# Macaron block (feed-forward, attention, feed-forward): bias row, gamma and beta scaled on ScalarE, and the bias of the first six tiles added in two transfers

## What is computed

```python
x = x + 0.5 * ffn(_layernorm(x))
x = x + attn(_layernorm(x))          # 16 heads of 32, causal
x = x + 0.5 * ffn(_layernorm(x))

# ffn(x):
z = x_flat @ ternary_quant(W_syn).T + b_syn        # 2048 hidden units
topv, _ = jax.lax.top_k(z, k)                      # k = 204 of 2048 in each row
hidden = jnp.where(z >= topv[:, -1:], jax.nn.relu(z), 0.0)
out = hidden @ ternary_quant(W_out).T + b_out
return layernorm(x + out, gamma, beta)
```

## Time and profile before

| | |
|---|---|
| median of 3 runs | 1203.69 us (1200.65 to 1203.73) |
| the profiled execution | 1203.05 us |
| its span, first to last instruction | 1201.3 us |
| mean granted clock of TensorE, share of full | 0.969 |
| busy: TensorE, VectorE, ScalarE, GpSimd | 88%, 74%, 67%, 31% |
| bias transfers | 32 of 1024 KB, median 8.0 us from issue to landing |

### The profile page before, as it was taken

The page is one execution under the profiler, slowest core; times in us unless marked ns, Lnnn a source line. Parts: engine busy times, 40 slices in busy tenths (PEclk is TensorE's granted clock), DMA queues, the critical chain, the costliest instruction groups (busy, mean ns, idle before and its releaser), DMA issues. The chain is left out here.

```text
span 1201.3 us, 17848 instructions
## 1 busy us (share of the span) xinstructions
PE 1059.9 (88%) x5862; PEld 476.8 (40%) x5862; DVE 890.0 (74%) x2207; ACT 803.6 (67%) x1193; POOL 376.2 (31%) x406
## 2 busy tenths in 40 slices
PE   0677899998889789999999699999999799998886
PEld 0233455554444333232244233232344345554443
DVE  4867899999985787885243787884225889999893
ACT  5368988898743546566713556667646988999762
POOL 1311254544554041100220041102211134544456
PEclk9898899998999989999999989999999899999999
DMA  9445333233000225200001143210043433344000
GB/s 367 126 89 102 71 71 58 54 67 67 27 1 1 53 63 115 54 37 2 1 4 36 36 101 77 54 37 2 1 83 76 88 71 71 72 88 89 19 19 35
DMA packets 28105, 74.62 MB, mean 62 GB/s; under 512 B 5332, under 2 KB 7767, under 8 KB 23255
## 3 DMA queue, kind: packets, MB, share of 16 engines
q0 software_dynamic: 7456, 39.33, 17.5%
q1 hardware_dynamic: 20536, 33.99, 8.9%
HBM read 56.37 MB, written 4.21 MB: 50 GB/s over the span
## 5 line engine op out<-in xcount | busy, mean ns | idle before, releaser
L859 ACT ACTIVATE arena<-arena,X 128x2048 int8<-128x2048 f32 x154 | 307.9, 2005 | 18.3 <-issue 10.4
L919 ACT ACTIVATE arena<-zP,asc 128x512 f32<-128x512 f32 (+3 forms) x384 | 200.7, 582 | 110.9 <-PE zP L706 80.0
L549 PE MATMUL zP<-T,arena 128*128 128x512 f16 x1024 | 248.1, 393 | 0.0
L597 PE MATMUL oP<-T,arena 128*128 128x512 f16 x832 | 199.9, 384 | 0.9 <-DVE arena L1438 0.9
L549 PEld LDWEIGHTS zP<-T,arena 128*128 128x128 f16 x1024 | 103.3, 101 | 125.6 <-issue 16.9
L815 ACT ACTIVATE arena<-zP,sc 128x512 f32<-128x512 f32 x128 | 87.0, 686 | 69.9 <-PE zP L549 69.7
L597 PEld LDWEIGHTS oP<-T,arena 128*128 128x128 f16 x832 | 81.7, 99 | 80.2 <-issue 6.3
L702 PE MATMUL zP<-arena 98*128 98x512 f16 (+3 forms) x384 | 110.8, 334 | 0.9 <-ACT arena L919 0.7
L1124 POOL TENSOR_TENSOR arena<-arena 128x512 f32<-128x512 f32 x16 | 20.3, 1271 | 257.7 <-DVE arena L1582 235.9
L1552 DVE CUSTOM_DVE_ANT_0 scored<-hP,causal 128x128 bf16<-128x128 f32 (+3 forms) x170 | 80.9, 485 | 21.5 <-PE hP L681 20.2
L681 PE MATMUL hP<-arena 96*128 96x512 f16 (+3 forms) x256 | 83.6, 345 | 14.3 <-DVE mx L1552 11.0
(11 more groups left out here) (206 smaller groups left out, 1797.6 us busy)
## 6 DMA issues: line engine op xcount, KB each, us to landing
arena<-bz_row POOLq DMA_DIRECT2D x32, 1024.0 KB, 8.0
arena<-arena SPq DMA_DIRECT2D x168, 64.0 KB, 2.0
arena<-in_w_synT SPq DMA_DIRECT2D x4, 1024.0 KB, 8.1
arena<-in_w_outT SPq DMA_DIRECT2D x4, 1024.0 KB, 14.9
x_sb<-in_b_o POOLq DMA_DIRECT2D x2, 2048.0 KB, 17.9
out_dram<-x_sb SPq DMA_DIRECT2D x16, 256.0 KB, 2.0
x_sb<-in_x SPq DMA_DIRECT2D x3, 1024.0 KB, 13.9
arena<-in_w_o SPq DMA_DIRECT2D x2, 1024.0 KB, 5.2
```

Of the source, the lines that this page charges most:

```text
L549: mm = pe.matmul(zP[:, c * CW:(c + 1) * CW], part[:, g % 2, k, :], T1[:, k, c * CW:(c + 1) * CW], start=(n == 0 and k == 0), stop=(n == 1 ...
L597: mm = pe.matmul(o, part[:, k, :], T2[:, k, :], start=(c == 0 and n == 0 and k == 0), stop=False)
L859: act.activation(junk[:, counted[0] % 2, :], Z[:, g % ZR, :], ACT.Sign, bias=X[:, 2, k:k + 1], accum_out=S[:, k:k + 1]).then_inc(sm["cnt"], 1)
L919: act.activation(PT[:, m // 4 % 2, h, q0:512], colP[m % 3][:, q0:512], ACT.Exp, scale=asc[:, g, 10:11]).then_inc(sm["exp_done"], 1)
```

## The change

The bias row, gamma and beta are scaled by ScalarE instead of GpSimd: gamma and beta ahead of the absolute sum of the last weight piece, the bias row behind the sum of squares. For the first six tiles of pass 0 the bias is added in two transfers: columns 0 to 1535 (chunks 0 to 2) as soon as three chunks are evacuated, issued ahead of the root of that slot, and columns 1536 to 2047 one slot later, ahead of the next first part. From tile 6 on everything is as before. The semaphore `z_set` becomes two, for even and odd tiles.

```diff
+        SPLIT_BIAS = 6
+        def bias_parts_of(g):
+            return ((0, 3), (3, 4)) if g < SPLIT_BIAS else (None, (0, 4))
+        def z_ready(g):
+            mine = range(g % 2, g + 1, 2)
+            return sm[f"z_set{g % 2}"], 16 * sum(2 if m < SPLIT_BIAS else 1 for m in mine)
...
                 for c in range(4):
+                    if (n, c) == (1, 3):
+                        act.wait_ge(sm["vec_in"], 32)
+                        for v in (gam, bet):
+                            act.activation(v[:, :], v[:, :], ACT.Copy, scale=0.5).then_inc(sm["vec_set"], 1)
                     act.wait_ge(sm[f"w{n + 1}_in{c}"], 16)
...
             act.wait_ge(sm["sq_done"], 1)
+            act.wait_ge(sm["bsyn_in"], 16)
+            act.activation(bz, bsyn[0:1, :], ACT.Copy, scale=SH[0:1, :]).then_inc(sm["bz_set"], 1)
...
-            def add_bias(f, i):
-                g = f * NT + i
-                if (f, i) == (0, 0):
+            def add_bias(f, i, part):
+                g = f * NT + i
+                if not bias_parts_of(g)[part]:
+                    return
+                lo, hi = bias_parts_of(g)[part]
+                if (g, part) == (0, 0):
                     pool.wait_ge(sm["bz_out"], 16)
-                pool.wait_ge(sm["z_evac"], 4 * g + 4)
-                pool.dma_start(Z[:, g % ZR, :], bz_row.partition_broadcast(P), accum_op=ALU.add).then_inc(sm["z_set"], 16)
+                pool.wait_ge(sm["z_evac"], 4 * g + hi)
+                cols = slice(lo * CW, hi * CW)
+                pool.dma_start(Z[:, g % ZR, cols], bz_row[cols].partition_broadcast(P), accum_op=ALU.add)\
+                    .then_inc(sm[f"z_set{g % 2}"], 16)
...
                     do(final, f, s, S_FIN + 1)
+                    if f == 0 and s - 2 < SPLIT_BIAS:
+                        do(add_bias, f, s, 2, 1)
                     do(rstd2, f, s, S_FIN)
+                    late = f * NT + s - 1 >= SPLIT_BIAS
+                    if not late:
+                        do(add_bias, f, s, 1, 0)
                     if f == 0 or s > 0:
                         do(rstd1, f, s, -1)
-                    do(add_bias, f, s, 1)
+                    if late:
+                        do(add_bias, f, s, 1, 1)
                     if f == 0 and s == 0:
-                        pool.wait_ge(sm["scales_set"], 1)
-                        pool.tensor_scalar(bz, bsyn[0:1, :], SH[0:1, :], None, ALU.mult).then_inc(sm["bz_set"], 1)
 
                         pool.wait_ge(sm["scales_set"], 3)
                         pool.tensor_tensor(SIG, sc[:, 16:17], half[:, :], ALU.pow).then_inc(sm["scales_set"], 1)
-                        link(pool.tensor_scalar(gam[:, :], gam[:, :], 0.5, None, ALU.mult))
-                        link(pool.tensor_scalar(bet[:, :], bet[:, :], 0.5, None, ALU.mult))
+                        pool.wait_ge(sm["vec_set"], 2)
```

More of the change, by code:

```diff
@@ L294, in program @@
                  "ones_set ident_set consts_set abs_done sum_ps sum_read tern_done sq_done scales_set search_set "
-                 "bz_set bz_out z_set orow_in bcol_in bpart_set brow_out bones_set "
+                 "bz_set vec_set bz_out z_set0 z_set1 orow_in bcol_in bpart_set brow_out bones_set "
                  "stats1 xn_done rstd1 xT_ps xT_hi xT_lo z_ps z_evac upd cnt below_set ok_set ok_sum ok_read "
@@ L851, in count @@
                     act.wait_ge(sm["search_set"], 1)
-                    act.wait_ge(sm["z_set"], 16 * (g + 1))
+                    act.wait_ge(*z_ready(g))
                 if s >= FIRST_UPD:
@@ L1330, in count_here @@
                 g = f * NT + i
-                dve.wait_ge(sm["z_set"], 16 * (g + 1))
+                dve.wait_ge(*z_ready(g))
                 after(0)
```

## The result

The changed kernel takes 1189.95 us (median, 1188.85 to 1190.24) against 1202.72 for the kernel before, run beside it: ratio 0.9897 with a 95% interval of 0.9885 to 0.9909. Its profiled span is 1187.0 us (before 1201.3), its mean granted clock 0.978 (before 0.969). The forecast was 1192.3 in a range of 1189 to 1198. Run a second time, beside another set of the kernel before, it took 1191.97 (1188.7 to 1194.8), ratio 0.9911 (0.9896 to 0.9927). So the gain is 10.9 to 12.8 us; 11.4 was forecast. It is small, 1.0% of the time, but both intervals leave out 1.

The account below looks back on a forecast made before the run. The first slots' chain was taken as the bound: VectorE's stall beside GpSimd's scaling, then counts waiting for bias transfers. 5.8 + 5.4 = 11.2 us off 1203.05 gives 1191.9, from the median 1192.5; forecast 1192.3, range 1189 to 1198.

Parts of the forecast that it names:

- The stall goes: Start-up: `normal` of tile 1 no longer held beside GpSimd's scaling; 5.77 us gained at the transposes of tile 2.
- the charge of gamma and beta: Start-up: scaling them on ScalarE takes 1.3 us and delays the first `mm1` by some 0.8 us, beside `normal`.
- Slot 2: VectorE's `update` starts directly behind `normal` at 58.5, no longer waiting for the count: 1.2 us gained, 6.97 in all.
- no delay, 0.8 to spare: Slot 2: the part ahead of tile 3's root is issued by 56.1; the root wants to start at 56.9.
- rival 1: Slots 2 to 4: root behind the evacuation costs more, matmuls at TensorE's lower level; 3.6 us lost, 1197, chance 0.17.
- Slots 3 to 6: Waits for the count go: slot 3 gains 2.62, slot 4 0.46, slot 5 nothing, slot 6 1.15; 11.2 in all.
- The transfers: Bias transfers, issue to landing: a quarter 4.0 us, three quarters 6.7 us (estimates), landing before ScalarE needs them in slot 2.
- rival 4: Slots 5 and 6: TensorE idles less and keeps its higher level; 2 to 3 us more gained, 1189.5, chance 0.07.
- Rival 3: Five slots: GpSimd's issues held up by VectorE push the root; 27 us lost against 11.2, 1219, chance 0.04.
- Rival 2: Only the start-up pays, bias landing as late as now: 1197.9, or 1200.8 if that saving is halved; chance 0.05.

Follow-up runs that it names:

- e5: Changed kernel with the bias row alone scaled on GpSimd again in one instruction, gamma and beta staying on ScalarE: 1194.87 us, ratio 0.9934.
- e13: Changed kernel with gamma and beta scaled behind the bias row instead of ahead of the last absolute sum: 1191.33 us, one run.
- e3: Changed kernel with the bias split after two chunks instead of three, two transfers of 1024 columns (halves): 1189.97 us, ratio 0.9888.
- e9: Changed kernel with the bias split after one chunk instead of three, 256 KB ahead and 768 KB behind: 1190.29 us, ratio 0.9899.
- e4: Changed kernel with the first bias part issued behind the root instead of ahead of it: 1191.50 us, ratio 0.9904.
- e8: Changed kernel without an edit, timed and profiled again: 1191.97 us, ratio 0.9911.
- the second profiles: Changed kernel and kernel before, each profiled once more without an edit: 1191.97 us (ratio 0.9911) and 1203.60 us (one run).
- e2: Changed kernel with bias row, gamma and beta scaled on GpSimd again, keeping only the two bias transfers: 1199.51 us, ratio 0.9970.
- e10: Changed kernel with bias in halves and tile 2's mean, variance, root and normalize moved ahead of the search's start values: 1194.03 us, ratio 0.9924.
- e1: Changed kernel with the bias of every tile in one transfer again, keeping only the scaling on ScalarE: 1197.57 us, ratio 0.9951.
- e11: Changed kernel with the bias row scaled on GpSimd in two instructions of 1x1024: 1192.18 us, one run.
- e6: Changed kernel with the bias row scaled on GpSimd in four instructions of 1x512: 1192.45 us, ratio 0.9918.

## Why the prediction was right, and where not

**The stall goes: right, 0.39 too small.** 5.77 was summed, 6.16 came. e5 shows that the bias row alone carries 5.35 of it at the transposes of tile 2, and 4.3 of the 10.66 at slot 7. `x_lo` of tile 1 was at 41.06 (forecast 41.3), the charge of gamma and beta 0.56 (forecast 0.8) and hidden, which e13 confirms. The bias row took 2.00 us on ScalarE (forecast 1.91). By the Trainium skill, "ScalarE: Activation LUTs", section What ACT_TABLE_LOAD costs, an instruction with one pointer operand takes about 280 ns and 0.833 ns for each element, 1.99 us for the row (an estimate by that page); the trace agrees with 2.00.

**Slot 2: the term that was off.** The step "no delay, 0.8 to spare" failed. The 32 matmuls took 8.35 us at a granted clock of 0.82, behind 2.92 us of idle time; chunk 2 was evacuated at 56.4 instead of 55.1, and the root of tile 3 started at 57.29 instead of 56.9 and read 0.35 longer. The slot gained 0.24 (6.16 to 6.40) where 1.20 was forecast. That is rival 1's mechanism in one slot, not in three, and it cost 1.0 us, not 3.6. e3 shows which part of it the root's wait costs. Its window of the same stretch has the same clock; its transposes take 1.11 us and its 32 matmuls 8.08:

```profile
49.80:58.50 8.70, 8.58 (x35) 4.15 (x36) 5.69 (x8) 4.29 (x6) 1.97 (x4) 0.82 0.66 120
```

```profile
49.92 1.11 PE L543 MATMUL xP<-identf,arena 128*128 128x128 f32 x4 [3.32 <-DVE arena L1301]
...
51.70 0.69 DVE L1307 SCALAR_TENSOR_TENSOR arena<-xP,arena 128x512 f16<-128x512 f32 x1 [1.84 <-ACT arena L800]
```

Its roots wait for two chunks only, and its `update` comes at 58.45, 0.62 earlier than in the changed kernel. So the root behind chunk 2 costs 0.6 of the 1.0 us. The rest stands before it: in e3 `x_lo` starts 1.78 us behind the start of the transposes (49.92 to 51.70) where it was 1.32 before (56.07 to 57.39), since the transposes run at the lower level, and the forecast had not counted that. That 58.45 agrees with the forecast of 58.5 is luck, the start-up's extra 0.39 against this. e9 is the case at the upper level: its transposes take 0.66 us, its 32 matmuls 7.07, behind 2.29 us of idle time, and its `update` comes at 58.24:

```profile
49.97 0.66 PE L543 MATMUL xP<-identf,arena 128*128 128x128 f32 x4 [2.29 <-DVE arena L1301]
50.47 7.07 PE L560 MATMUL zP<-T,arena 128*128 128x512 f16 x32
```

The prediction had set 2.28 us of idle time in the kernel before, followed by 7.07, against rival 1. Behind 2.43 us (e4) and 2.81 (e8) the 32 matmuls took 8.8, so that argument didn't reach as far as the 2.9 us at hand.

**Slots 3 to 6: right within 0.15 each.** Gained 2.48, 0.52, 0 and 1.26; forecast 2.62, 0.46, 0 and 1.15. (By the forecast's own lengths, 10.70 and 10.2, slot 4 is 0.50.) In slot 4 the root stood behind an issue as predicted. The closeness is in part that of one profile: the forecast was built on the first profile of the kernel before, and by the second profiles the four slots gained 2.35, 0.91, 0.27 and 1.37.

**The transfers: size off, with little consequence.** A quarter was to take 4.0 us and three quarters 6.7. Three quarters took 6.4 to 7.5, a quarter 5.1 to 7.1. The quarter is in flight together with a transfer of three quarters, and e9's first quarter, which is alone, took 4.34; that the company is the cause is argued from this. One wait of 0.80 in slot 3 is what is left of it, 0.17 of which reached VectorE. The line of the transfer:

```profile
L1088 POOL DMA_DIRECT2D arena<-bz_row x38: 853/947/1248, 46.1 to 1085.1; - x38
...
DMA to landing us min/median/max: 5.1/7.9/9.8
```

By the rule of the Trainium skill that the prediction weighed ("DMA: Bandwidth & Descriptors", anatomy of one DMA) a quarter would take 2.6 us (an estimate by that page); no run here shows one under 4.3.

**Parts that are not independent: not foreseen.** The sum treated the slots as following the start-up whatever it was. e2 shows that the two transfers alone lose 1.4 us that the new place of gamma and beta saves. That the scaling alone loses 1.6 is not shown, since the kernel before varies by as much.

**The end.** 1203.05 - 10.9 at the end of the first pass would be 1192.1, and the second set of runs gave 1191.97. The first set, 1189.95, has some 2 us more. The forecast had nothing for the part behind slot 7. There, 1.3 us (second pair of profiles) to 2.5 us (first pair) were gained between the two passes, and 1.5 us came or went with one slot, from the update of slot 8 to that of slot 9, in single executions. So the nearness of 1192.3 to the medians is in part luck: the first slots gained 10.7 by the profile that the forecast was built on and 12.2 by the other pair, and the late stretch adds what no step had. Whether the change shifts the mean clock by a little, as rival 4 has it, stays open; rival 4 had named slots 5 and 6, and nothing came there.

Rival 3, GpSimd's issues held by VectorE, did not come: no issue of the 38 took over 1.25 us (one each of e3 and e10 took 1.50). Rival 2 is excluded by e1 against the changed kernel: the two transfers are worth 6.3 us at slot 7 and 5.6 to 7.6 in the medians.

## What to carry to other kernels

Read an instruction that takes ten times its usual time for what runs beside it: here a one-partition instruction on GpSimd held VectorE for nearly its whole length. Moving it to an idle engine gave all of it back, cutting it into pieces most of it. When a large transfer behind the last of several producers is on the chain, send what is complete and keep the late part small, but cut so that the issue doesn't hold what is queued behind it; in the profiles here halves did that better than three quarters. Issuing more transfers early is no gain in itself: with three in flight (e10), the one that was needed first landed 10.3 us after its issue, where halves otherwise took 4.9 to 6.6. And profile the kernel before twice before dividing a gain into parts: here two of its profiles differed by 1.5 us at slot 7, as much as the part in question.

## What was not expected of the hardware

- A GpSimd instruction on one partition holds a VectorE instruction by 0.3, 0.72 and 5.1 us for 512, 1024 and 2048 elements, while it runs 1.58, 2.87 and 5.47 us itself. Held were `normal` on 128x512, which has one tile as input, a sum of two on 128x4 (e11), and two casts on 128x4 and an instruction on 128x1 (e6). The Trainium skill, "GPSIMD Engine Reference", section Specifications, names contention at the shared interfaces for VectorE instructions with two SBUF inputs or in a 2-port mode. The sum of two agrees; in which mode the others ran, no trace here shows.
- An accumulating transfer onto 128 rows took, in the first slots, 4.3 to 8.0 us for 256 KB, 4.9 to 6.6 for 512 KB, 6.2 to 8.3 for 768 KB and 7.7 to 8.6 for 1024 KB, and 10.3 and 10.9 for 512 KB with two others in flight (e10).
- The first instruction of a root reads 0.57 us where its record begins 0.29 us before that of the issue ahead of it ends (57.29), 0.25 where it begins 0.04 behind that end (66.09), and 0.22 behind a wait for VectorE.
- The same program was granted 0.91 and 0.99 of TensorE's clock in the same 50 us of two executions, and one slot there took 15.2 and 16.7 us.
